# A transformer layer on one core: the engines' lists in a new order, DVE's dependent steps set apart, one subtraction moved from DVE to GpSimd

## What is computed

```python
h = _layernorm(x) * (1 + ca) + sa
x = x + ga * attention(h)     # rmsnorm, q/k/v, causal softmax, sigmoid gates per head, Wout
h = _layernorm(x) * (1 + cb) + sb
x = x + gb * ffn(h)
# ffn: sim = q . keys (4 heads, two halves of 64 keys), top 8 of each half,
#      the 8 best sums of pairs choose among 512 experts;
#      w = silu(h . down_embed[idx]) * softmax(scores); experts = sum w * up_embed[idx]
#      out = (silu(h Wg + bg) * (h Wu + bu)) Wd + bd + experts
```

## Time and profile before

| | |
|---|---|
| time, median of 3 runs | 1450.23 us (1448.07 to 1450.8) |
| span of the profiled execution | 1448.7 us; the page lists no time of its own for it beside the span |
| TensorE busy | 1399.7 us, 97% |
| DVE busy | 1289.4 us, 89% |
| ScalarE busy | 1270.9 us, 88% |
| GpSimd busy | 1052.9 us, 73% |
| mean granted TensorE clock | 0.995 |
| DMA | 7.1% of 16 engines' span for the main queue, 19 GB/s |

### The profile page before, as it was taken

How to read it: one execution, slowest core, us unless ns; L and a number is a source line. 1 busy time by engine, 2 the same in 40 slices (tenths; PEclk the granted TensorE clock), 3 DMA queues, 4 the chain that set the end, 5 groups by cost and what they waited for, 6 DMA issues and landing times.

```text
span 1448.7 us, 39838 instructions
## 1 busy us (share of the span) xinstructions
PE 1399.7 (97%) x11491; PEld 1161.5 (80%) x11491; DVE 1289.4 (89%) x5345; ACT 1270.9 (88%) x4212; POOL 1052.9 (73%) x1221
## 2 busy tenths in 40 slices
PE   6899999999999999999999999999999999999998
PEld 4678788888788888788888788888788888788887
DVE  5589999999999999999999999999999999999977
ACT  6788988898988898988898988898988898988885
POOL 2048787778787777787777787787787777777760
PEclk9999999999999999999999999999999999999999
DMA  4000000000000000000000000000000000000000
GB/s 132 16 14 21 15 10 20 20 16 20 13 11 20 20 16 20 14 10 20 20 16 20 13 11 20 20 16 20 15 9 20 20 16 20 14 10 24 10 14 10
DMA packets 51041, 27.74 MB, mean 19 GB/s; under 512 B 10336, under 2 KB 50208, under 8 KB 51008
## 3 DMA queue, kind: packets, MB, share of 16 engines
q1 hardware_dynamic: 50768, 26.91, 7.1%
q10 hardware_dynamic: 240, 0.43, 0.1%
HBM read 23.02 MB, written 4.31 MB: 19 GB/s over the span
## 4 chain that ended last, share of the span: by engine, by line
PE 81%; ACT 14%; issue 3%; DVE 1%; DMA 0%; SPq 0%; POOL 0%; ACTq 0%; DVEq 0%; POOLq 0%
PE pW L1457 10%; PE pS L1527 9%; PE pW L1540 9%; PE pW L1568 8%; PE pW L1459 8%; PE pW L1458 8%; PE pS L1517 7%; PE pS L1513 6%; PE pW L1613 4%; PE pW L1610 4%; ACT pT L652 4%; ACT pS L660 4%; PE pW L1544 3%; PE pW L1601 2%; ACT h L750 2%
## 5 line engine op out<-in xcount | busy, mean ns | idle before, releaser
L660 ACT ACTIVATE pS<-pS,nmx 128x128 f32<-128x128 f32 (+1 forms) x1024 | 389.4, 433 | 33.2 <-DVE nmx L1085 33.2
L1085 DVE CUSTOM_DVE_ANT_0 pS<-pS,mask 128x128 f32<-128x128 f32 (+1 forms) x1024 | 331.8, 390 | 27.2 <-PE pS L1517 22.7
L504 POOL TENSOR_TENSOR fexp<-fexp,fsum 128x512 f32<-128x512 f32 x240 | 299.9, 1284 | 76.6 <-DVE fexp L1214 76.6
L652 ACT COPY pT<-pS 128x768 f32<-128x768 f32 x256 | 216.1, 844 | 42.2 <-PE pS L1527 40.4
L495 POOL TENSOR_TENSOR fsum<-ex 128x512 f32<-128x512 f32 x248 | 250.6, 1047 | 0.0
L1527 PE MATMUL pS<-ident,p_sb 128*128 128x128 f32 x1536 | 216.3, 277 | 6.1 <-DVE p_sb L1105 4.2
L1105 DVE TENSOR_TENSOR p_sb<-pS,coef 128x256 f32<-128x256 f32 (+2 forms) x512 | 210.5, 453 | 8.9
L1527 PEld LDWEIGHTS pS<-ident,p_sb 128*128 128x128 f32 x1536 | 173.7, 141 | 37.3 <-issue 18.9
L660 ACT ACTIVATION_READ_ACCUMULATOR pS<-pS,nmx 128x1 f32 x1024 | 193.7, 189 | 0.0
L642 ACT COPY qk<-pW 128x512 f32<-128x512 f32 x256 | 162.2, 634 | 4.6 <-PE pW L1459 1.1
L1540 PE MATMUL pW<-pT,v 128*64 128x256 f32 x1024 | 165.9, 402 | 0.3 <-ACT pT L652 0.2
(11 more groups left out here) (211 smaller groups left out, 3696.1 us busy)
## 6 DMA issues: line engine op xcount, KB each, us to landing
x_in<-in_L_attn_tokens SPq DMA_DIRECT2D x32, 128.0 KB, 2.1
x_res<-in_L_attn_tokens SPq DMA_DIRECT2D x32, 128.0 KB, 3.0
modB<-mods_dram SPq DMA_DIRECT2D x32, 128.0 KB, 2.9
modA<-mods_dram SPq DMA_DIRECT2D x31, 128.0 KB, 3.1
out<-yo SPq DMA_DIRECT2D x31, 128.0 KB, 1.9
modC<-mods_dram SPq DMA_DIRECT2D x32, 64.0 KB, 3.2
fsum<-in_L_attn_Wkv SPq DMA_DIRECT2D x1, 512.0 KB, 6.0
w_out<-in_L_attn_Wout SPq DMA_DIRECT2D x1, 512.0 KB, 7.2
```

What stands on the lines that cost most here:

```text
L504: ins = nc.gpsimd.tensor_tensor(fexp[:, k, h, :], fexp[:, k, h, :], fsum[:, k, h].rearrange("p i j -> p (i j)"), ALU.mult)
L652: nc.scalar.copy(pT[:, p % 2], pS[:, p % 2, :, 0:SW]).then_inc(S(pT_ready), 1)
L660: ins = nc.scalar.activation(ps, ps, ACT.Exp, bias=nmx[:, p % 2, h, k:k + 1], scale=-1.0, accum_out=den(p)[:, h, k:k + 1])
L1085: ins = nc.vector.tensor_tensor_reduce(out=ps, in0=ps, in1=mask[:, (1 - k) * P:2 * P], scale=-1.0, scalar=LARGEST, op0=ALU.add, op1=ALU.mi ...
```

## The change

The change does four things.

1. The common lists of TensorE, ScalarE, DVE and GpSimd are written in a new order, and `order`, which deals the banks, follows it. The jobs of pass 0 and of batch 0 and 1's first products get a deal of their own (`opening`, with semaphores `open_full` and `open_free`), as the drained ones at the end had before.
2. DVE's chains are cut into single steps, each with its signal and its wait as separate calls: `normalise` into `invert`, `coefficients`, `normalise`; `thresholds` into `top_candidates`, `sum_top`, `invert_top`; `ln1_stats` and `ln1_modulate` into `stats1`, `aggregate1`, `center1`, `scale1`, `shift1`, `square1`; `ln2_stats` into `gate_attention`, `add_residual`, `stats2`, `aggregate2`; `shift` into `row_largest` and `shift`; `finish` into `gate_output` and `finish`. Other work can stand between two of them.
3. The subtraction `top_d` of the common passes moves from DVE to GpSimd (`shift_top`, last in its list). `products(k)` waits for `ex_ready[k]`.
4. `row_max` signals after each head instead of after both, and `exp_scores` waits for each head.

```diff
+        order = [("GU", 1, -2), ("D", 0, -2), ("V", 0, 0), ("PV", 6, -1), ("PV", 7, -1), ("V", 3, 0), ("QK", 2, 0),
+                 ("V", 4, 0), ("QK", 3, 0), ("QK", 4, 0), ("D", 1, -2), ("QK", 5, 0), ("V", 5, 0), ("GU", 2, -2),
+                 ("V", 1, 0), ("op", 0, -1), ("QK", 6, 0), ("GU", 3, -2), ("PV", 0, 0), ("PV", 1, 0), ("PV", 2, 0),
+                 ("hT", 0, -1), ("PV", 3, 0), ("QK", 7, 0), ("ET", 0, -2), ("V", 2, 0), ("sim", 0, -1),
+                 ("sim", 1, -1), ("PV", 4, 0), ("PV", 5, 0), ("xT", 0, 1), ("y", 0, -2), ("ET", 1, -2),
+                 ("GU", 0, -1), ("QK", 0, 1), ("QK", 1, 1)]
...
+                def shift_top():
+                    if w.live(-1):
+                        pool.wait_ge(S(head_chain), at(head_chain, f, 4))
+                        if w.live(-2):
+                            pool.wait_ge(S(tops_ready), at(tops_ready, g, 1))
+                        kh = TB * RH
+                        nc.gpsimd.tensor_tensor(top_d[:, :, :, :], top_s[:, :, :, :], top_s[:, :, :, 0:1].broadcast_to([P, 2, kh, TK]),
+                                                ALU.subtract).then_inc(S(top_d_ready), 1)
...
+                products(0)
                 candidates()
-                products(0)
                 products(1)
+                rstd1()
+                add_bias()
                 weigh(0)
-                add_bias()
                 add_heads(0)
                 fold(0)
                 rstd2()
+                rms1()
                 weigh(1)
-                rstd1()
                 add_heads(1)
-                rms1()
                 fold(1)
+                shift_top()
...
-                        ins.then_inc(S(max_ready), 1)
-
-                def normalise(p):
+                            ins.then_inc(S(max_ready), 1)
+
+                def invert(p):
+                    if w.live(0):
+                        dve.wait_ge(S(exp_ready), at(exp_ready, i, p + 1))
+                        nc.vector.reciprocal(den(p), den(p)).then_inc(S(inverse_ready), 1)
```

More of the change, by code:

```diff
@@ L186, in program @@
         drain_free = [sem(f"drain_free{n}") for n in range(NW)]
+        open_full = [sem(f"open_full{n}") for n in range(NW)]
+        open_free = [sem(f"open_free{n}") for n in range(NW)]
         per = {}
@@ L219, in program @@
         h2_ready = ev("h2_ready", 1)
+        ex_ready = [ev(f"ex{k}_ready", 1) for k in range(TB)]
         top_d_ready, tops_ready = ev("top_d_ready", 1), ev("tops_ready", 1)
@@ L695, in gate_up @@
                         w.wait_full("GU", c)
+                        if c == 0 and w.has("y") and not (isinstance(i, int) and i == B):
+                            w.wait_full("y")
                         bank = w.bank("GU", c)
@@ L1017, in _ @@
             su_link(nc.vector.tensor_copy(cT[:, :], pW[0][:, 0:B]))
-            modulate1(0)
+            center1(0)
+            scale1(0)
+            shift1(0)
+            square1(0)
             def split_qkv(pieces):
@@ L1098, in normalise @@
                         ins.then_inc(S(coef_ready), 1)
+                def normalise(p):
+                    if w.live(0):
                         dve.wait_ge(S(coef_ready), at(coef_ready, i, p + 1))
[L1100 to L1101 removed]
                         mine = slice(0, 1) if p in SHARED else slice(0, 2)
@@ L1224, in finish @@
                         nc.vector.tensor_tensor(o, o, modC[:, 0:1, :].broadcast_to([P, TB, D]), ALU.mult).then_inc(S(y_gated), 1)
+                def finish():
+                    if w.has("y"):
                         dve.wait_ge(S(y_gated), at(y_gated, g, 1))
@@ L1278, in body @@
                     row_max(5)
+                    invert(4)
+                    coefficients(4)
                     normalise(4)
+                    invert(5)
+                    coefficients(5)
                     normalise(5)
-                    ln1_modulate()
+                    ln1(center1)
+                    ln1(scale1)
+                    ln1(shift1)
+                    ln1(square1)
                     row_max(6)
@@ L1366, in body @@
                     return
-                thresholds()
+                top_candidates()
+                ln1(stats1)
+                bias_product(1)
+                ln1(aggregate1)
+                gate_product(1)
+                sum_top()
+                gated_down(0)
                 row_max(0)
+                invert_top()
+                row_max(1)
+                ln1(center1)
                 choose(0, 0)
                 choose(0, 1)
-                row_max(1)
+                invert(0)
@@ L1374, in body @@
+                ln1(scale1)
+                coefficients(0)
+                invert(1)
                 normalise(0)
-                bias_product(1)
-                gate_product(1)
+                coefficients(1)
                 normalise(1)
-                gated_down(0)
+                ln1(shift1)
+                gated_down(1)
                 choose(1, 0)
-                gated_down(1)
                 row_max(2)
                 row_max(3)
+                invert(2)
+                coefficients(2)
@@ L1392, in body @@
                 row_max(4)
                 row_max(5)
+                invert(4)
                 low_part(h2T_high, h2T, "hT")
+                coefficients(4)
                 normalise(4)
+                invert(5)
+                coefficients(5)
+                normalise(5)
+                row_largest(0)
+                row_largest(1)
                 shift(0)
-                normalise(5)
-                ln1_modulate()
+                row_max(6)
                 shift(1)
-                row_max(6)
+                invert(6)
@@ L1401, in body @@
+                coefficients(6)
                 row_max(7)
+                normalise(6)
+                invert(7)
+                coefficients(7)
                 low_part(xT_high, xT, "xT")
-                normalise(6)
+                gate_output()
                 finish()
                 bias_product(0)
+                gate_product(0)
                 normalise(7)
-                gate_product(0)
                 if first:
```

341 lines of the change are left out of this document (196 added, 145 removed), and 8 rows, old and new, of tables (opening, order).

## The result

The changed kernel takes 1404.07 us (median of 4 runs, 1400.69 to 1407.57) against 1449.15 us (median of 4, 1445.3 to 1450.8): ratio 0.9693, 95% interval 0.967 to 0.9717. The forecast was 1437 us with a range from 1416 to 1478.

A forecast was written before the change was run, and what follows sets the result against it. The order in which the engines' lists meet was taken as the bound, no engine's work alone. Floor 42.5 plus 0.5 gave 43.0 us per pass against 43.43, -13 us over 30 passes: 1437 us, range 1416 to 1478.

The forecast's parts named there:

- Waits of before: TensorE's lost time at scores(3) to output projection (0.20), QK 4 (0.36) and scores(5) (0.47): 1.03 us per pass, removable by reordering.
- This pays only where a wait for DVE ends last: Shortening DVE from 39.8 to about 37 us per pass gains only there, as DVE is not the slowest engine.
- Price of the borders: TensorE's cost where unlike products meet: +0.1 us per pass, bounds -0.5 and +0.5, as grouping would earn nothing.
- The floor: TensorE's pass without its old waits: 42.4 us, or 42.5 with the +0.1 for borders between unlike products.
- rival 2: Few holds bite and TensorE's list alone sets the pass: 42.5 us, time 1422; chance 0.15.
- GU 3 waits +0.5: GU 3 waits for gate_product(2)'s bank, delayed by choose(1,0)'s held masks; free at 8.6 against 8.1 us: +0.5 per pass.
- The slack ahead of V 1: DVE frees V 1's bank through gated_down(1) after 9.5 us, TensorE arrives at 10.3: 0.8 spare, enough for one hold.
- The race of scale1: After the last mask step DVE's scale1 should issue narrowly before GpSimd's weighing: 0.03 to 0.12 against 0.08 us.
- rival 1: scale1 is held 1.05 us, V 1 starts 1.25 and GU 3 0.6 late: 44.35 per pass, 1477; chance 0.25.
- The subtraction: Moved to GpSimd's list end, it takes 0.3 to 1.3 us (0.45 taken), delays nothing and counts as nothing.
- DVE from 39.8 to about 37: DVE's time per pass falls through the removed subtraction (1.34 us) and dependent steps set apart (0.85 to 1.9).
- Rivals 3 and 4: New waits at y, QK 1, GU 3: 1447 to 1453, chance 0.12; an unseen wait: 1453 to 1465, chance 0.06.

## Why the prediction was off, step by step

**Waits of before, 1.03 us per pass.** Right: the earlier trace rows's three waits are gone. The kernel with old lists shows that the new order is what removes them, and the joined steps and the single signal show that the order alone doesn't: DVE and ScalarE follow it only with early signals and spaced steps. "This pays only where a wait for DVE ends last" was true of the old order; in the new one it is worth 37 and 85 us. I had given these steps no price there, and so did not see that they carry the forecast.

**Price of the borders, taken at +0.1 with bounds -0.5 to +0.5.** This is the step that failed. The floor went from 42.4 to 41.87: the term was -0.53, past its lower bound, where I had +0.1. I compared GU 1 with QK 0 and counted runs of three-part projections, nine and nine. What the runs price are half-array stretches: nine in the old pass and six in the new. The range then made it worse, as it took in only 0.2 of the bound of 0.5: rival 2 with the whole of it is 42.4 - 0.5 = 41.9 per pass, and 1448.7 - 1.53 x 30 + 1.5 = 1404 us. Here the Trainium skill's rule (TensorEngine Tiling (Array Packing), Key Properties), that a change of tiling mode drains TensorE, said that grouping would earn something, and the runs side with it against my count. Three stretches fewer at 0.35 are 1.05. Against them stand two changes more between scores and value products inside stretches, by the rows above about 0.17 each (a stretch of scores 4 and value product 2 takes 1.66, twice that 3.32; two scores and two value products in one stretch take 2.98, and 1.51 + 1.45 = 2.96 in two of them), and the layer's output, now in two parts, which takes 3.67 against 3.49 before (TensorE's timeline, 743.73 to 747.22). 1.05 - 0.34 - 0.18 = 0.53, and the floor went from 42.4 to 41.87, 0.53. That it closes to the hundredth is luck: the 0.35 is measured at one place, and a stretch behind a turned pair costs 0.17 in that pair where V 3 paid 0.09. It also leaves terms out, which TensorE's timeline of the kernel after shows:

```profile
713.64 0.44 PE L1594 MATMUL pW<-ident,xr 128*128 128x128 f32 x2
713.93 1.16 PE L1731 MATMUL pW<-w_d,g_t 128*128 128x128 f32 x8
...
715.82 0.60 PE L1722 MATMUL pW<-ident,d_t 128*128 128x128 f32 x4
716.17 0.36 PE L1580 MATMUL pW<-h2T_high,s_g_high 128*128 128x256 f32 x1
...
716.96 1.05 PE L1731 MATMUL pW<-w_d,g_t 128*128 128x128 f32 x8
...
718.74 0.82 PE L1648 MATMUL pS<-ident,p_sb 128*128 128x128 f32 x6
719.45 0.35 PE L1580 MATMUL pW<-xT_high,s_qkv_high 128*128 128x256 f32 x1
```

xT, ET 1 and y together take 2.53 + 1.78 = 4.31 here, against 4.35 before (742.87 to 747.22), as xT and ET 1 became cheaper by what y lost; so the 0.18 is no cost of its own. T 6 takes 0.71, against 0.57 before (748.72). With these the sum is 1.05 - 0.34 + 0.04 - 0.14 = 0.61 against 0.53. The stretches are the largest term by this count; the division among the terms isn't shown by a run.

**GU 3 waits +0.5.** Right place, wrong size: 0.15 to 0.2 in the rows, 0.10 as the difference of the two passes (41.97 and 41.87). choose(1,0) is held by 1.3 where I had 1.85 (2.32 against my 2.9), and the bank comes free 7.9 us after the turn of pair 0, not 8.6. Of the 1.03 us between the forecast's 43.0 and the measured 41.97, 0.40 is this term and 0.63 the floor (42.5 to 41.87).

**The slack ahead of V 1, 0.8.** Too large. The terms that I listed for DVE add up to 8.6 to 9.3 and not to 8.5, and in the kernel after V 1 starts only 0.24 behind the end of gated_down(1) (733.50 against 732.58 + 0.68). It didn't show since shift1 was held by 0.12 and not by the 0.65 that I had let fit in. That is luck: in the run with value product 7 alone shift1 is held by 1.0, and V 1 waits.

**The race of scale1.** Right, by 0.06 us, and the later place of scale1 shows what losing it costs: 1441.5, not rival 1's 1477. The rival was counted from a floor 0.63 too high, and its waits of 1.85 came to 1.35 (that run's pass takes (1356.48 - 103.10) / 29 = 43.22). The Trainium skill's rule (SBUF — State Buffer, Who interferes with whom), whoever issues first blocks the other, agrees: scale1 takes 0.40 when it starts 0.06 ahead of GpSimd's product, and 1.25 when it comes behind it.

**The subtraction.** Right in all: 0.40 on GpSimd, nothing waits for it, and it earns nothing.

**DVE from 39.8 to about 37.** Measured 37.3 per pass.

**The rivals.** Rival 2, TensorE's list alone, is what happened in kind; its 1422 has the same wrong floor. With 41.87 it would have been 1448.7 - 1.56 x 30 = 1402 of span. Rivals 3 and 4 did not come.

**Open.** Which of the chains joined in one step (thresholds ahead of pair 0, or the coefficient of pair 3) costs the 35 us was not separated. That each of the three stretches saved is worth 0.35 was worked out from neighbours, not run one by one. Why T 6 takes 0.14 more in its new place, and why the end of the kernel is shorter by 3.7 us, was not looked into.

## What to carry to other kernels

Where TensorE is the bound, count its changes of array use (half against whole, and which half) in the order of work, and price one by starting times across a lone block and a paired one: here 0.35 us for the one that was measured, and 0.53 for all changes of TensorE's own time, a third of the 1.46 us gained per pass. A feature that earns nothing when added alone can be what carries a new order; test it by taking it out of the new kernel too. And before trusting a delay to be small, look whether it pushes a DVE step past the end of one GpSimd product and into the next: 0.36 us became 1.2.

## What the hardware showed that was not expected

- Splitting a pair of half-array products by a projection cost 0.35 us of TensorE time at the place measured: 0.16 in the two products, 0.09 in the one ahead of the lone product and 0.10 in the one behind.
- Holds between DVE and GpSimd are two-sided: the four weighing products took 5.02 in the earlier trace rows and 5.58 here, with held DVE steps between them; on DVE's side a hold of one step was anything from 0.1 to 1.0.
- Delays of tenths of a microsecond gave five kernels almost one time (1441.2 to 1441.7) by different routes: V 1's bank, GU 3's bank or scores(5). Why they agree so closely isn't shown.
